# Routing and tile loop of a two-layer mixture of experts: slots ahead of the expert table, gathers ahead of scatters, both picks in one product

## What is computed

```python
logits = xt @ Wr + br
probs = jax.nn.softmax(logits, axis=-1)
top_p, top_idx = jax.lax.top_k(probs, 2)
weights = top_p / top_p.sum(axis=-1, keepdims=True)
xe = xn[None, :, :] * ln_g[:, None, :] + ln_b[:, None, :]
h = gelu(jnp.einsum('end,edh->enh', xe, W1) + b1[:, None, :])
y = jnp.einsum('enh,ehd->end', h, W2) + b2[:, None, :]
out = (weights[:, :, None] * sel).sum(axis=1)     # sel: y of the two picked experts
x = x + out
```

## Time and profile of the kernel before

| | us |
|---|---|
| median of three executions | 1781.64 |
| the three | 1776.52, 1781.64, 9649.8 |
| the profiled execution | 1780.64 |
| its span in the trace | 1778.9 |
| mean granted TensorE clock | 0.981 of full |

### The profile page before, as it was taken

One profiled execution on the slowest core, in us unless ns is written; L12 is line 12 of the kernel. 1 busy time (PEld: TensorE's weight loads), 2 busy tenths in 40 slices (PEclk: granted clock), 3 DMA queues, 4 the chain that ended last, 5 costly groups with the idle time before them and its releaser, 6 DMA issues.

```text
span 1778.9 us, 41264 instructions
## 1 busy us (share of the span) xinstructions
PE 1647.1 (93%) x13276; PEld 1519.3 (85%) x13277; DVE 904.0 (51%) x2170; ACT 1025.8 (58%) x2334; POOL 356.4 (20%) x318
## 2 busy tenths in 40 slices
PE   4799999999799999588999999999988999999998
PEld 3578888888688889478999999999978999999997
DVE  4578878777511112478878888877760111111111
ACT  1143444445355556258989999899734455554443
POOL 2110000000166656330000000000012333333332
PEclk9899999999999999799999999999998999999999
DMA  9990000024387878500000000000365666666663
GB/s 161 107 177 10 10 10 9 22 76 166 98 204 195 214 182 195 163 6 22 13 15 19 9 19 13 15 20 12 131 254 187 179 180 182 187 186 179 177 178 97
DMA packets 93536, 190.33 MB, mean 107 GB/s; under 512 B 20777, under 2 KB 67625, under 8 KB 84617
## 3 DMA queue, kind: packets, MB, share of 16 engines
q1 hardware_dynamic: 60745, 139.50, 23.6%
q0 software_dynamic: 31360, 48.69, 17.2%
q10 hardware_dynamic: 1344, 1.05, 0.2%
HBM read 189.22 MB, written 33.22 MB: 125 GB/s over the span
## 4 chain that ended last, share of the span: by engine, by line
PE 52%; DVE 3%; DMA 1%; issue 1%; ACT 1%; POOL 0%; ACTq 0%; DVEq 0%; SPq 0%; POOLq 0%
PE bank L1783 24%; PE bank L2311 12%; PE bank L2350 11%; PE bank L713 1%; PE bank L716 1%; DMA X<-xd 1%; PE bank L2318 1%; ACT arena L1485 1%; DVE arena L1621 0%; DMA arena<-xs,slot_row 0%; PE bank L2191 0%; DVE arena L1619 0%; PE bank L703 0%; PE bank L2198 0%; PE bank L2181 0%
## 5 line engine op out<-in xcount | busy, mean ns | idle before, releaser
L1783 PE MATMUL bank<-arena 128*128 128x195 bf16 x5408 | 466.5, 248 | 15.1 <-DVE arena L1621 10.8
L1783 PEld LDWEIGHTS bank<-arena 128*128 128x128 fp8e4 x5408 | 463.3, 97 | 18.4 <-issue 17.4
L1485 ACT ACTIVATE arena<-arena,m_row 128x512 fp8e5<-128x512 f32 (+1 forms) x672 | 401.5, 678 | 43.8 <-DVE arena L1621 31.4
L2430 DVE TENSOR_TENSOR arena<-bank,X 128x256 f32<-128x256 f32 x118 | 50.1, 424 | 585.0 <-PE bank L2350 585.0
L2311 PEld LDWEIGHTS bank<-X,arena 128*128 128x128 f32 x2832 | 337.9, 194 | 7.7 <-issue 1.7
L2311 PE MATMUL bank<-X,arena 128*128 128x128 f32 x2832 | 338.8, 277 | 0.6 <-DMA arena<-m0w 0.6
L2350 PE MATMUL bank<-arena,X 128*128 x1416 | 329.3, 383 | 7.4 <-ACT X L2403 7.1
L1325 PE MATMUL bank<-arena 128*128 (+1 forms) x1352 | 312.1, 386 | 15.1 <-DVE arena L1231 15.0
L1325 PEld LDWEIGHTS bank<-arena 128*128 128x128 f32 x1352 | 252.5, 191 | 55.7 <-issue 20.8
L2350 PEld LDWEIGHTS bank<-arena,X 128*128 128x128 f32 x1416 | 260.7, 191 | 44.2 <-issue 12.7
L1183 ACT ACTIVATE bank<-arena,s_all 128x384 f32<-128x384 f32 (+1 forms) x234 | 133.7, 573 | 184.9 <-DVE arena L1223 183.2
(11 more groups left out here) (253 smaller groups left out, 1336.6 us busy)
## 6 DMA issues: line engine op xcount, KB each, us to landing
arena<-m1w SPq DMA_DIRECT2D x67, 1024.0 KB, 12.3
arena<-m0w SPq DMA_DIRECT2D x67, 512.0 KB, 7.7
arena<-qd SPq DMA_DIRECT2D x25, 256.0 KB, 3.2
arena<-adjT POOLq DMA_DIRECT2D x13, 448.0 KB, 12.8
arena<-adjT POOLq DMA_DIRECT2D x13, 384.0 KB, 10.8
xs<-X SPq DMA_DIRECT2D x14, 256.0 KB, 2.6
xe<-zeros POOLq DMA_DIRECT2D x1, 3456.0 KB, 21.7
X<-x_in SPq DMA_DIRECT2D x2, 1664.0 KB, 11.4
```

The source lines that it names most:

```text
L1485: last = a.activation(self.sign[slot].bitcast(F8W)[:, q * W:q * W + nt * P], self.row[r][:, 0:nt * P], ACT.Sigmoid, scale=STEEP, bias=self ...
L1783: last = pe.matmul(bank[rb * NT + n][:, kind * KW:(kind + 1) * KW], self.split[slot][kind].bitcast(F8)[:, q * W + n * P:q * W + (n + 1) * ...
```

## The change

- `pick1` and `pick2` get a common name `picks` (they lie side by side); both are multiplied by `posx` in one instruction, and one reduction gives all 52 slot numbers. Tile and place come from f32 arithmetic: adding and subtracting `ROUND` rounds to multiples of 128, so `tile_of` is the tile's first slot, and the iotas that it is compared with count in steps of 128 too. The sums in bank 5 then hold row numbers without the former factor.
- `tile_table()` is called behind the instruction that writes `slot_row`, no longer in front.
- SyncE loads only the first W1 once the table is known (it waited for the slots as well, which now lie ahead), the second once the first gather has landed, b2 once the second has.
- GpSimd issues gather 4 in front of its loop, and in the loop `gather(g + 5)` where `gather(g + 4)` was.
- TensorE waits for the table only in front of the down products.

```diff
--- before.py
+++ after.py
@@ -68,10 +68,10 @@
 IN_VALUES = 6
 EARLY_PAIR = 8
 ROW = D + 4
-SECOND_CODE = 32
-SECOND = SECOND_CODE * P
+SECOND = 32 * P
 GROUP = 2
 CHUNKS = ((0, 7), (7, 14), (14, 20), (20, 26))
+ROUND = 1.5 * 2 ** 23 * P
 PICK_PARTS = ((0, 20), (20, T))
 EARLY_GROUPS = 4
 SIDES = (0, 12, T)
@@ -1824,6 +1824,7 @@
                 TE = T * E
                 self.logits = words(k, TE)
                 k += TE
+                self.picks = words(k, 2 * TE)
                 self.pick1 = words(k, TE)
                 k += TE
                 self.pick2 = words(k, TE)
@@ -1866,16 +1867,14 @@
                 self.turn_banks = turn_banks
                 self.row_cols = words(k, 4 * T).rearrange("p (t c) -> p t c", c=4)
                 k += 4 * T
-                self.slot_i = words(k, 2 * T).bitcast(I32)
+                self.slot_no = words(k, 2 * T)
                 k += 2 * T
-                self.part_i = words(k, 4 * T).bitcast(I32)
-                k += 4 * T
+                self.slot_tile = words(k, 2 * T)
+                k += 2 * T
                 self.tile_of = words(k, T).bitcast(BF16)
                 k += T
                 self.place_of = words(k, T).bitcast(BF16)
                 k += T
-                self.slots = words(k, SLOT_TILES)
-                k += SLOT_TILES
                 self.scale_x = words(k, T)
                 k += T
                 if second_norm:
@@ -2065,16 +2064,14 @@
                 step(v.tensor_tensor(p3, i3.rearrange("p e t -> p t e"), w3, ALU.subtract))
                 step(v.tensor_tensor(p3, p3, spread_t(self.base, T), ALU.add))
                 step(v.tensor_tensor(self.posx, bank[3][:, 0:TE], self.posx, ALU.add))
-                for k, pick in enumerate((self.pick1, self.pick2)):
-                    step(v.tensor_tensor(self.work, self.posx, pick, ALU.mult))
-                    step(v.tensor_reduce(self.best, w3, AXX, ALU.add))
-                    step(v.tensor_copy(self.slot_i[:, k * T:(k + 1) * T], self.best))
-
-                step(v.tensor_scalar(self.part_i[:, 0:2 * T], self.slot_i, 7, None, ALU.logical_shift_right))
-                step(v.tensor_scalar(self.part_i[:, 2 * T:4 * T], self.slot_i, P - 1, None, ALU.bitwise_and))
-                step(v.tensor_copy(self.tile_of, self.part_i[:, 0:2 * T]))
-                step(v.tensor_copy(self.place_of, self.part_i[:, 2 * T:4 * T]))
-
+                both = self.picks.rearrange("p (k n) -> p k n", k=2)
+                step(v.tensor_tensor(both, both, self.posx.rearrange("p (o n) -> p o n", o=1).to_broadcast([P, 2, TE]),
+                                     ALU.mult))
+                step(v.tensor_reduce(self.slot_no, self.picks.rearrange("p (t e) -> p t e", e=E), AXX, ALU.add))
+
+                step(v.tensor_scalar(self.slot_tile, self.slot_no, P / 2 - 0.5, ROUND, ALU.subtract, ALU.add))
+                step(v.tensor_scalar(self.tile_of, self.slot_tile, ROUND, None, ALU.subtract))
+                step(v.tensor_tensor(self.place_of, self.slot_no, self.tile_of, ALU.subtract))
 
                 def weights():
 
@@ -2123,21 +2120,18 @@
                     tile = self.hot_tile[b][:, 0:groups * 2 * G * GROUP].rearrange("p (u m r) -> p u m r", u=groups, r=GROUP)
                     v.tensor_tensor(tile[:, :, 0:G, :], eq, columns(self.codes, G), ALU.mult
                                     ).then_inc(self.hot_ids[b], 1)
-                tile_table()
-
                 for k in range(2):
                     v.wait_ge(self.hot_used[k], 3)
 
-                slots = self.slots
                 codes, places = bank[5][:, 0:G], bank[5][:, G:2 * G]
-                v.tensor_scalar(slots, codes, float(P), None, ALU.mult)
-                step(v.tensor_scalar(slot_w[:, :], codes, float(SECOND_CODE), None, ALU.is_ge))
-                step(v.tensor_tensor(slots, places, slots, ALU.add))
-                step(v.tensor_scalar(self.spare, slots, 0.0, spare_row[:, :], ALU.is_equal, ALU.mult))
+                v.tensor_scalar(slot_w[:, :], codes, float(SECOND), None, ALU.is_ge)
+                step(v.tensor_scalar(self.spare, places, 0.0, spare_row[:, :], ALU.is_equal, ALU.mult))
+                step(v.tensor_tensor(self.spare, codes, self.spare, ALU.add))
                 step(v.scalar_tensor_tensor(out=self.spare, in0=slot_w[:, :], scalar=-float(SECOND), in1=self.spare,
                                             op0=ALU.mult, op1=ALU.add))
-                v.scalar_tensor_tensor(out=slot_row[:, :], in0=slots, scalar=1.0, in1=self.spare,
+                v.scalar_tensor_tensor(out=slot_row[:, :], in0=places, scalar=1.0, in1=self.spare,
                                        op0=ALU.subtract, op1=ALU.add).then_inc(self.slots_ready, 1)
+                tile_table()
 
             def route_scalar(self, a, last_gelu=None):
                 def turned(i):
@@ -2226,11 +2220,11 @@
             def route_gpsimd(self, pool, rows_final):
                 pool.wait_ge(*rows_final)
                 pool.wait_ge(self.lg_done, T // 2)
-                pool.iota(self.tile_all, [[1, SLOT_TILES], [0, GROUP]], base=0, channel_multiplier=0,
+                pool.iota(self.tile_all, [[P, SLOT_TILES], [0, GROUP]], base=0, channel_multiplier=0,
                           allow_small_or_imprecise_dtypes=True).then_inc(self.places_ready, 1)
                 pool.iota(self.place_all, [[1, P], [0, GROUP]], base=0, channel_multiplier=0,
                           allow_small_or_imprecise_dtypes=True).then_inc(self.places_ready, 1)
-                pool.iota(self.codes, [[SECOND_CODE, 2], [1, T]], base=0, channel_multiplier=0,
+                pool.iota(self.codes, [[SECOND, 2], [P, T]], base=0, channel_multiplier=0,
                           allow_small_or_imprecise_dtypes=True).then_inc(self.places_ready, 1)
 
             def tiles_sync(self, sp, w1m, b1m, b2m, next_weights=None):
@@ -2241,13 +2235,12 @@
                     sp.dma_start(self.W1[s], w1m[:, at(e * size, size)]).then_inc(self.w1_loaded[s], 16)
 
                 sp.wait_ge(self.tiles_known, 1)
-                for s in range(2):
-                    load_w1(s, s)
-                sp.wait_ge(self.slots_ready, 1)
+                load_w1(0, 0)
                 if not self.second_norm:
                     sp.dma_start(self.b1, b1m).then_inc(self.b_loaded, 16)
-                for s in range(2):
-                    sp.wait_ge(self.rx_loaded[s], 16)
+                sp.wait_ge(self.rx_loaded[0], 16)
+                load_w1(1, 1)
+                sp.wait_ge(self.rx_loaded[1], 16)
                 sp.dma_start(self.b2, b2m.partition_broadcast(P)).then_inc(self.b_loaded, 16)
 
                 def load_pair(i):
@@ -2284,14 +2277,18 @@
                 pool.wait_ge(self.slots_ready, 1)
                 pool.wait_ge(self.rows_stored, self.n_stored)
                 pool.wait_ge(self.cols_stored, 16)
+                def gather_behind_turn(g):
+
+                    pool.wait_ge(self.tx_ready[g % 2], g // 2 + 2)
+                    gather(g + 4)
+
                 for g in range(4):
                     gather(g)
                 pool.wait_ge(*total_ready)
+                gather_behind_turn(0)
                 for g in range(RUN_TILES):
-                    if g + 4 < RUN_TILES:
-
-                        pool.wait_ge(self.tx_ready[g % 2], g // 2 + 2)
-                        gather(g + 4)
+                    if g + 5 < RUN_TILES:
+                        gather_behind_turn(g + 1)
                     pool.wait_ge(self.ry_ready[g % 2], g // 2 + 2)
 
                     if n_to == 1 and g > 0:
@@ -2319,7 +2316,6 @@
                                             ident[:, :])
                     last.then_inc(self.tx_ready[q % 2], 1)
 
-                pe.wait_ge(self.tiles_known, 1)
                 pe.wait_ge(self.rx_ready, 1)
                 turn_x(0)
                 pe.wait_ge(self.rx_ready, 2)
@@ -2327,6 +2323,7 @@
                 turn_x(1)
                 pe.wait_ge(self.w1_loaded[0], 16)
                 hidden(0)
+                pe.wait_ge(self.tiles_known, 1)
                 pe.wait_ge(self.w2_loaded, 16 * 8)
                 def tile(j, q):
                     i, s = 2 * j + q // 2, q % 2
```

## The result

The changed kernel takes 1762.31 us (median of four, 1760.55 to 1765.26) against 1783.22 for the kernel before (median of four, which counts the single execution of 9649.8 us; without it 1781.64). The ratio leaves that execution out: 0.990, 95% interval 0.9878 to 0.9921, some 18 us. The forecast was 1756 in a range of 1746 to 1769. The span of the profiled execution is 1761.9 us against 1778.9.

A forecast was written before the change was run, and what follows sets the result against it. TensorE, busy 93% of the span, was taken as the bound, with gather waits stretching layer 0's loop. Savings of 5.5 + 3.0 + 16.5 = 25.0 us from 1781.64 gave 1756.6, stated as 1756, range 1746 to 1769.

The forecast's parts named there:

- What bounds the loop: Layer 0's tile loop: ScalarE's waits for gathers stretch it; gathers one tile further ahead save 16.5 us, at most 18.3.
- the floor of 3.73 us: Layer 0's tile interval: 1.785 for up products, 1.73 for down products and 0.21 for transposes, against 4.05 measured.
- The rival that scatters or the DMA engines hold the loop: Layer 0's loop stays at about 3.9 us per tile, giving back 8.6 us instead of 16.5: 1764; chance 0.19.
- The routing: Routing stage: five steps take 1.9 us instead of 2.95, and slot rows are ready 1.8 us sooner in each layer.
- Layer 1's first up product: Start of layer 1's tiles: up products begin 5.5 us sooner (bounds 4.5 and 6.6), with W1(0) arriving last.
- The start of layer 0: Start of layer 0's tiles: first gelu waits for b2, first down product 3.0 us sooner (bounds 2.0 and 4.0).
- the sum of 25.0: Total saving in us: 5.5 at layer 1's start, 3.0 at layer 0's start and 16.5 in layer 0's loop.
- Both are needed only 3.6 us or more after the up products start: Layer 1's start: W1(1) and b2, loaded behind the first and second gathers, are needed no sooner than that.
- The rival that the first gathers stay contended: Both starts: second gather may take 6 us, saving 3.6 instead of 5.5 in layer 1, 1 less in layer 0: 1759; chance 0.10.
- The clock: Both starts: gain from a higher granted clock put at 0, far bounds 2.5 us (layer 1) and 1.3 (layer 0).

The follow-up runs named there:

- w1_late: The changed kernel with both first W1 loads issued only when the first two gathers have landed, b2 behind them; ratio to the kernel before 0.9919.
- b1_alone: The changed kernel with b1 and b2 on semaphores of their own, so the gelus wait for b1 only; ratio to the kernel before 0.9893.
- loop_alone: The kernel before with only GpSimd's order changed: gather(g + 5) issued where gather(g + 4) was; ratio to the kernel before 0.9925.
- loop_undone: The changed kernel with GpSimd's order of the kernel before, gather(g + 4) in front of scatter(g); ratio to the kernel before 0.998.
- sync_old: The changed kernel with both first W1 loads issued as soon as the table is known, as before; ratio to the kernel before 0.9913.
- b2_early: The changed kernel with b2 in a place of its own, loaded during the routing behind the store of the columns; ratio to the kernel before 0.9916.
- after_again: The changed kernel executed a second time, with nothing changed; ratio to the kernel before 0.9906.
- b1_idle70: `b1_alone` with 70 idle products on TensorE behind the last chunk instead of 40; ratio to the kernel before 0.9896.

## Why the prediction was right, point by point

- **What bounds the loop: right.** 18.3 us were expected at most and 16.5 taken, 15.7 came. The term stands on the waits at L2379 and the floor of 3.73 us worked out from layer 1. The waits vanish with the edit alone and come back without it, and the median interval is 3.73. The margin between 3.78 and 3.73 lies in a few intervals of 3.9 to 4.42, the longest in the middle, where the next layer's weights are loaded; TensorE's listed waits for W1 are small (1.7 us at the weight loads, 0.4 at the products).
- **The rival that scatters or the DMA engines hold the loop: did not happen**, and not by much to spare either: the share of the DMA engines rose from 0.79 to 0.84, and VectorE waited for a scatter once, 3.2 us, without stopping TensorE.
- **The routing: right.** 1.94 us for five steps (1.9 forecast), slot rows 1.78 and 1.79 us sooner (1.8).
- **Layer 1's first up product: right in size** (5.6 for 5.5), **wrong in what comes last.** I had W1(0) landing at 1334.1 to 1335.2 behind rows ready at 1333.9; in the run the rows set it, 2.1 us behind the second `norm`, since the second gather took 4.05 us instead of 3.0. It was close: by its semaphore in the trace W1(0) landed 24.47 us behind the counts, 5.3 us after its issue and within the forecast's bounds, 0.13 us before the first up product. The size was no luck, then; which of the two came last was nearly a tie. The Trainium skill's 4.4 us for 1 MB (DMA: Bandwidth & Descriptors, Anatomy of one DMA; an estimate from a fit for DMAs issued from GpSimd, and SyncE issues this one) named the rows as last, which came true only because the gather was slow: the load took 5.3 us here and 5.1 in `w1_late`.
- **The start of layer 0: the step that failed.** It was to be 3.0 us shorter and was 1.8 us longer: 4.8 of the 6.1 us by which the stretches miss the sum of 25.0. The path was right (the first gelu waits for b2), and three of its sizes were wrong, which add up to the 4.8. First, b2 went out 23.5 us behind the counts instead of 22.1, 1.3 later, with the second gather. Second, b2 took 7.9 us to land. I used the 4.7 that it took in the kernel before, where it goes out when both W1 loads have landed, and allowed at most 1.5 more (1.0 in the value taken) for its going out while they are in flight; the 7.9 are 2.2 us more than I took (7.5 to 8.9 over both layers and both executions). Third, "1.3 us for gelu" runs from the gelu's start to the down product, but the gelu starts 1.24 us behind b2's landing (474.54 + 7.90 = 482.44 against 483.68). The trace of the kernel before shows that gap already: 474.10 + 4.8 = 478.9 against 480.12.

```profile
474.10 0.36 SPq L2251 DMA_DIRECT2D X<-m0b  x1
...
480.12 1.14 ACT L2403 ACTIVATE X<-bank,arena 128x128 f32<-128x128 f32 x4 [2.64 <-PE bank L2311]
```

The gap is 1.23 us in the kernel before and 1.23 or 1.24 in the seven other executions in which layer 0's first gelu follows b2, also where the profile names another releaser. "Both are needed only 3.6 us or more after the up products start" failed for b2 in layer 1 too, but cost little there (0.7 us by `b1_alone`).
- **The rival that the first gathers stay contended: half right.** One load costs the second gather 1.1 to 1.5 us (2.9 and 2.8 against 4.05 and 4.3), not the 3 us of that rival. The 5.7 us that I took from the earlier trace rows as the most that a gather takes was too low: the row has not all landings, and by its `norm` the second gather of layer 1 took 7.8 us in the kernel before (issued at 1330.38, normalised at 1338.18). The rule of the Trainium skill cited there (same page, Queues, rings and completion order), that an engine takes turns between its queues, agrees with what the runs show: in layer 0 the first gather is ready 2.9 us behind its issue with a load behind it or without (`w1_late`), and the ones issued close to the load are slowed.
- **The clock: put at 0, and small.** The first 32 up products of layer 0 took 5.65 us instead of 4.87, the first 64 of layer 1 8.95 instead of 9.69. Kept up by more idle products the clock brings 1.5 us at layer 0's start (1.3 was the price) and 1.4 at layer 1's (2.5; the first up product came 0.6 us later in that run); in layer 0 it is given back at once.

## What to carry to other kernels

When a queue alternates between a prefetch and a result that has to wait, look at which of the two the consumer waits for: moving the prefetch one tile ahead costs nothing if the buffer is already free, and here it was worth most of the change (13 us of some 18 by the ratios). When transfers are put in a new order, don't carry a landing time over from a profile in which the transfer was alone: sum the bytes that are in flight when it is issued, and ask who waits on its semaphore. A semaphore shared by two loads makes every reader wait for the later one; here the gelu needed only the 16 KB of b1 and waited for 1 MB. And measure from the landing to the work that waited for it: 1.2 to 1.3 us of loop entry and look-up stood behind this wait.

## What was not expected of the hardware

- The time of a small, scattered store differs between executions: the 3328 pieces of 16 bytes took 5.5 to 5.9 us in the first profiled executions of both kernels and in the four variants of one chip (`loop_alone`, `loop_undone`, `b1_alone`, `sync_old`), and 6.2 to 7.9 in the others, on other chips. In some of those it, and not the slot rows, released the gathers, with a 1 MB load beside it (`b2_early`) or without (`after_again`).
- In the two starts a gather took 2.9 us with no load beside it, 4.05 with a 1 MB load issued 0.7 us behind it, and 6.4 with one issued 0.2 us behind it and b2, in flight since 9 us, landing 0.5 us after its issue.
- In `b1_idle70` a stretch of 4.4 us of which TensorE was busy 1.9, with one pause of 2.5, was followed by a granted clock of 0.51 for 3.5 us.
